# A projection issued one step earlier and a SiLU issued three steps later in a fused graph and Mamba kernel

## The reference

```python
h = layernorm(x) @ W_fc1.T + b_fc1
u, z = split(h @ W_in.T)                      # 1024 channels each
u = silu(causal_conv4(u) + conv_b)            # 4 taps along the tokens
dt, B, C = split(u @ W_xproj.T)               # 32, 16, 16
delta = softplus(dt @ W_dt.T + b_dt)
h[t] = exp(delta[t] * A) * h[t-1] + (delta[t] * u[t]) * B[t]     # 16 states per channel
y[t] = sum_s h[t, s] * C[t, s] + u[t] * D
x = x + (y * silu(z)) @ W_out.T @ W_fc2.T + b_fc2
```

## Time and profile before

| what | value |
|---|---|
| median of 3 runs (lowest, highest) | 3827.84 us (3824.13, 3829.54) |
| the profiled execution, its own time | 3826.3 us |
| its span, first to last instruction | 3824.5 us |
| VectorE busy, share of the span | 3570.9 us, 93% |
| TensorE matmul busy | 3473.0 us, 91% |
| GpSimd busy | 3453.5 us, 90% |
| ScalarE busy | 2853.9 us, 75% |
| mean granted TensorE clock | 0.985 of full |

### The profile page before, as it was taken

The page is one execution under the profiler, slowest core; times in us unless marked ns, Lnnn a source line. Parts: engine busy times, 40 slices in busy tenths (PEclk is TensorE's granted clock), DMA queues, the critical chain, the costliest instruction groups (busy, mean ns, idle before and its releaser), DMA issues.

```text
span 3824.5 us, 43807 instructions
## 1 busy us (share of the span) xinstructions
PE 3473.0 (91%) x11130; PEld 1956.7 (51%) x11130; DVE 3570.9 (93%) x3133; ACT 2853.9 (75%) x6066; POOL 3453.5 (90%) x1860
## 2 busy tenths in 40 slices
PE   6789999999999999999999999999999999999888
PEld 3645555555555555555555555555555555555444
DVE  0399999999999999999999999999999999999998
ACT  1487777887777877777878777778777778777774
POOL 0199999999999999999999999999999999999998
PEclk9899999999999999999999999999999999999999
DMA  2111101111101111101111100111110111110110
GB/s 105 56 54 57 57 7 54 54 57 57 57 8 52 54 57 57 57 16 44 54 57 57 57 36 24 54 57 57 57 51 10 57 54 57 57 53 9 45 50 9
DMA packets 50702, 183.68 MB, mean 48 GB/s; under 512 B 7339, under 2 KB 33203, under 8 KB 42067
## 3 DMA queue, kind: packets, MB, share of 16 engines
q1 hardware_dynamic: 48880, 174.17, 11.8%
q10 hardware_dynamic: 1636, 7.83, 0.5%
HBM read 164.15 MB, written 17.83 MB: 48 GB/s over the span
## 4 chain that ended last, share of the span: by engine, by line
POOL 53%; issue 32%; PE 8%; DVE 4%; ACT 1%; POOLq 1%; DMA 0%; SPq 0%; DVEq 0%; ACTq 0%
POOL st L409 35%; POOL st L400 10%; POOL du_sb L390 3%; POOL delta L382 3%; PE y_ps L680 2%; PE g L700 2%; DVE st L863 2%; DVE st L851 1%; POOL rstd L348 1%; PE dec L617 1%; POOLq L189 1%; DVE u L889 0%; PE g L822 0%; DMA rows<-bk_dram 0%; PE dec L626 0%
## 5 line engine op out<-in xcount | busy, mean ns | idle before, releaser
L409 POOL TENSOR_TENSOR st<-st,bc 128x1024 f32<-128x1024 f32 x1024 | 2402.7, 2360 | 183.4 <-DVE st L863 178.9
L863 DVE TENSOR_TENSOR_SCAN st<-dec,st 128x1024 f32<-128x1024 f32 x1024 | 2330.5, 2289 | 36.1 <-ACT dec L462 28.8
L680 PE MATMUL y_ps<-st,ident 128*128 128x512 f32 x4096 | 1950.0, 608 | 250.5 <-POOL st L409 246.4
L462 ACT ACTIVATE dec<-delta,decay 128x254 f32<-128x254 f32 x4096 | 1697.1, 464 | 479.6 <-DVE st L863 475.9
L680 PEld LDWEIGHTS y_ps<-st,ident 128*128 128x128 f32 x4096 | 743.5, 191 | 1096.7 <-issue 621.4
L851 DVE TENSOR_TENSOR st<-du,bc 128x1024 f32<-128x1024 f32 x736 | 893.7, 1214 | 0.7 <-ACT du L448 0.6
L400 POOL TENSOR_TENSOR st<-du_sb,bc 128x1024 f32<-128x1024 f32 x288 | 679.6, 2360 | 0.1
L502 ACT ACTIVATE u<-d_ps,bconv,chan 128x256 f32<-128x256 f32 x256 | 130.1, 558 | 338.5 <-PE d_ps L718 332.3
L889 DVE SCALAR_TENSOR_TENSOR u<-d_ps,chan,u 128x250 f32<-128x250 f32 (+2 forms) x768 | 307.4, 473 | 59.2 <-ACT u L502 59.2
L718 PE MATMUL d_ps<-xnT,wxz 128*128 128x256 f32 x1024 | 256.5, 396 | 9.5 <-DVE u L889 8.7
L730 PE MATMUL d_ps<-xnT,wxz 128*128 128x256 f32 x1024 | 246.3, 383 | 15.0 <-ACT zs L513 14.4
(11 more groups left out here) (101 smaller groups left out, 2459.0 us busy)
## 6 DMA issues: line engine op xcount, KB each, us to landing
bc<-bc_dram SPq DMA_DIRECT2D x64, 2048.0 KB, 9.4
xg<-x_dram SPq DMA_DIRECT2D x32, 256.0 KB, 11.4
x_dram<-xg SPq DMA_DIRECT2D x32, 256.0 KB, 2.0
last_x<-x_dram SPq DMA_DIRECT2D x32, 256.0 KB, 2.6
out_dram<-last_x SPq DMA_DIRECT2D x32, 256.0 KB, 2.1
bc<-w_inT_dram ACTq DMA_DIRECT2D x1, 4096.0 KB
adjt<-adjT_dram SPq DMA_DIRECT2D x32, 128.0 KB, 11.1
bc<-w_out_dram ACTq DMA_DIRECT2D x1, 2048.0 KB
```

What stands on the lines that cost most here:

```text
L409: nc.gpsimd.tensor_tensor(st[:, sl, :, :, :], st[:, sl, :, :, :], bc[:, p, 1, SU * q:SU * q + SU, None, :].to_broadcast([P, SU, 2, T]), AL ...
L462: a = nc.scalar.activation(dec[:, v % 2, s, j, :].rearrange("p (b t) -> p b t", b=PAIR)[:, :, 1:], delta[:, p, 2 * i + j, :].rearrange("p ...
L680: mm = nc.tensor.matmul(y_all, ident[:, :], st[:, sl, s, :, :].rearrange("p j t -> p (j t)"), start=False, stop=(q == Q - 1 and s == SU - ...
L863: nc.vector.tensor_tensor_scan(h, dec[:, v % 2, :, :, :].rearrange("p s j t -> p (s j t)"), h, 0.0, ALU.mult, ALU.add).then_inc(S["scanned ...
```

## The change

u(0) of a group moves on TensorE from step 0 of a body to the end of step 31 of the body before, ahead of sum(30). It keeps its two waits. evac(i) and taps(i) keep their steps, for which a tuple `U_READY` of its own now stands. ScalarE's SiLU of z moves from step 3 to step 6, where it stands behind decays(7); step 7 begins with evac(3). No instruction is added or removed.

```diff
-U_STEPS = (0, 2, 4, 6)
+U_STEPS = (-1, 2, 4, 6)
+U_READY = (1, 3, 5, 7)
...
-SILU_U, SILU_Z = 10, 3
+SILU_U, SILU_Z = 10, 6
...
                 for v in range(U):
-                    if dense and v - 1 in U_STEPS:
-                        evacuate_u(act, k + 1, r, U_STEPS.index(v - 1))
+                    if dense and v in U_READY:
+                        evacuate_u(act, k + 1, r, U_READY.index(v))
...
                     if dense:
                         dense_pe(pe, k + 1, r, v, ends)
+                    if ends and v + 1 == U:
+                        first_u(pe, k + 2, p)
                     for step in graph_steps(k, p, v, ends, begins):
                         graph_pe(pe, *step)
...
+            def first_u(pe, g, r):
+
+                wait(pe, "xnT_made", g + 1)
+                wait(pe, "z_biased", J * g)
+                if isinstance(g, int) and g == 0:
+                    pe.wait_ge(S["folded"], FOLDS)
+                project_u(pe, g, r, 0)
+
+            def project_u(pe, g, r, i):
+
+                for j in (2 * i, 2 * i + 1):
+                    for c in range(KC):
+                        mm = nc.tensor.matmul(d_ps[:, j % 2, :], wxz[:, c, j * P:(j + 1) * P],
+                                              xnT[:, r, c, :], start=(c == 0), stop=(c == KC - 1))
+                mm.then_inc(S["u_mm"], 1)
+
             def dense_pe(pe, g, r, v, ends):
                 if v in U_STEPS:
-
                     i = U_STEPS.index(v)
-                    if i == 0:
-                        wait(pe, "xnT_made", g + 1)
-                        wait(pe, "z_biased", J * g)
-                        if isinstance(g, int) and g == 0:
-                            pe.wait_ge(S["folded"], FOLDS)
-                    else:
-                        wait(pe, "taps", CONV * g + 6 * i)
...
+                    wait(pe, "taps", CONV * g + 6 * i)
+                    project_u(pe, g, r, i)
...
             def conv(dve, g, r, v):
 
-                for i, start in enumerate(U_STEPS):
+                if v in U_READY:
                     for n in range(6):
-                        if v == start + 1:
-                            tap(dve, g, r, i, n)
+                        tap(dve, g, r, U_READY.index(v), n)
```

## The result

| what | before | after |
|---|---|---|
| median (lowest, highest) | 3827.32 us (3824.13, 3829.54), 4 runs | 3789.21 us (3787.34, 3790.81), 4 runs |
| profiled execution, its time (span) | 3826.3 us (3824.5) | 3789.18 us (3787.4) |

The ratio is 0.9901, 95% interval 0.9884 to 0.9918: 1% faster, against 3787 us forecast.

A forecast was written before the change was run, and what follows sets the result against it. VectorE's waits were taken to bound the kernel: 81.7 us before, 30 x 0.85 + 10 x 1.2 + 3.4 = 40.9 after. The 40.8 gain from 3826.3 gives 3785.5, plus 1.5 for the median: 3787 us, range 3768 to 3815.

The forecast's parts named there:

- VectorE sets the period: GpSimd waits for scans, level with VectorE at c(27), with at least 2.0 us to give; VectorE's savings shorten the period.
- u(0) fits ahead of sum(30): TensorE's idle 1.94 us ahead of sum(30) takes u(0)'s 1.89 without delaying that sum; gain 1.1 us at taps(0).
- The SiLU fits in step 6: ScalarE's table load and SiLU fit between decays(7) and evac(3); the 1.07 us wait at scan(5) goes.
- u(3) stops VectorE next: u(3) stays behind sum(4), which needs c(4); taps(3) waits 0.85 us, leaving VectorE a lead of about 1.35 us.
- The thin margins: taps(2), scan(8) and gate(0) hold by little: charged at nothing, each bounded at 0.3 us, 9 us over the bodies.
- The clock: TensorE's clock falls move ahead of sum(2), in about ten bodies; taps(3) comes 1.2 us later there than in other bodies.
- The last dense body: A clock fall at sum(4) holds taps(3), so nothing is gained there: 3.4 us of waits stay.
- The sum: VectorE's waits in the 31 bodies fall from 81.7 to 40.9 us, a gain of 40.8.

The follow-up runs named there:

- x_pad7: The changed kernel plus two spare statistics instructions on VectorE (0.65 us together) ahead of the taps of step 7; 3787.46 us, 0.9900 of the kernel before.
- e6_u3_ahead: The changed kernel with u(3) issued in step 5 ahead of sum(4), instead of step 6 behind it; 3789.33 us, 0.9907 of the kernel before.
- e2_silu_alone: The kernel before with only the SiLU moved to step 6, u(0) staying in step 0; 3786.43 us, 0.9901 of the kernel before.
- x_pad14: The changed kernel plus the same two spare VectorE statistics instructions, in step 14; 3820.83 us, 0.9986 of the kernel before.
- e1_u0_alone: The changed kernel with the SiLU back in step 3, so only u(0) is moved; 3792.31 us, 0.9919 of the kernel before.
- e7_out_spread: As e6_u3_ahead, plus the first block of the output projection in step 7 instead of 8; 3783.67 us, 0.9890 of the kernel before.
- e3_u2_step3: The changed kernel with u(2) on TensorE in step 3 ahead of sum(2), instead of step 4; 3792.26 us, 0.9914 of the kernel before.
- e9_hop_step3: The changed kernel with one graph hop on TensorE (6 matmuls, 1.3 us) moved from step 1 to step 3; 3779.65 us, 0.9881 of the kernel before.
- e10_hop_and_ahead: The hop move of e9_hop_step3 on top of e7_out_spread; 3761.72 us, 0.9834 of the kernel before.

## Why the prediction was right

- *VectorE sets the period.* Shown: spare work in step 14 costs at least its own length, and GpSimd still waits for scans.
- *u(0) fits ahead of sum(30).* It does, 0.23 us of idle are left ahead of the sum, and the wait at taps(0) is gone. The sum still starts with c(30), as forecast.
- *The SiLU fits in step 6.* It does; 2.0 us of ScalarE's idle time were forecast behind it, 2.09 measured. With the Trainium skill's figure for a table switch ("ScalarE: Activation LUTs", What ACT_TABLE_LOAD costs), about 1.3 us a body would have been lost; the trace shows no such drain, in step 6 as in step 7, and the measurement decides.
- *u(3) stops VectorE next.* 0.85 us forecast, 0.83 to 0.96 measured, and x_pad7 and e6_u3_ahead show that its place behind sum(4) is the cause. That c(4) alone sets that place is too simple: in the change the queue from sum(2) on, 2.64 us of waiting for c(2) behind it, reaches sum(4) at nearly the same moment. This is the step that made the forecast 3787 instead of some 3760.
- *The thin margins.* taps(2), scan(8) and gate(0) show no wait that the profile lists in ordinary bodies.
- *The clock.* Falls forecast in ten bodies ahead of sum(2): the ten of every third body and one more. Two sizes were off. The idle stretch is 2.64 us, not 1.95. The forecast's own rows give it: from 2127.1 to 2129.84 is 2.7 us, so the 1.95 was reckoned wrong, and the likeness to the 1.94 us that is filled was a slip too. And a fall costs 1.40 + 0.48 - 0.88 = 1.0 us more than an ordinary body, not 1.2. They hardly touch the sum, because only the count enters it. That the count stayed near ten was not understood: e2_silu_alone, e6_u3_ahead and x_pad14 have five, 29 and 19, at idle stretches that are the same or nearly so. The term 10 x 1.2 could as well have been 5 or 29 times, and the forecast was lucky in it: 29 falls would have put the time some 20 us higher.
- *The last dense body.* 3.4 us forecast to stay, because taps(3) hung on a fall at sum(4); 1.96 at taps(2) and 0.53 at gate(0) measured, and none at taps(3). The fall now comes at sum(2), so the reason given did not hold, and 0.9 us were gained.
- *The sum.* Forecast: waits from 81.7 to 40.9 us. Measured: 51.5 + 27.1 = 78.6 before (nineteen bodies wait 1.1 us at taps(0), not twenty, and one wait of 1.7 us of the 28.8 belongs to the start and stays) and 40.1 after, 38.5 us less, for 37.1 us between the two profiled executions.

What the prediction did not say, and e1 and e2 show, is that either part would have done. After the first one the cap of u(3) and the falls take nearly all that the second offers.

## What to carry to other kernels

When a wait on the bounding engine is removed, look for the next thing that this engine will meet and that does not move with it: here u(3) behind sum(4), which let VectorE keep 1.3 of the 2.17 us that it was early. Two edits that each gain up to the same cap are worth one of them; time them apart, and lift the cap before keeping both. Idle time that is filled on TensorE may open again a few steps later, so follow its queue to the next wait, and fill with work that waits for nothing itself: the moved hop took the falls away, the moved u(2) did not.

## What the runs showed of the hardware

The idle stretch alone does not say how often TensorE's clock falls. With about 2.6 us of idle ahead of sum(2) in every loop body, it fell in 10 bodies (x_pad7), 11 (the change), 13 (e1_u0_alone), 19 (x_pad14) and 29 (e6_u3_ahead and e7_out_spread). The falls keep a rhythm of bodies: every third one in the change, every fifth in e2_silu_alone, every second in the later part of e3_u2_step3, and every one in e6_u3_ahead and e7_out_spread, where the bodies follow at 112.6 to 112.7 us. What differs between the runs with equal stretches is the period of the bodies. That the period sets the rhythm is an inference; no run changed the period by itself.

The falls in the loop bodies follow idle stretches of 1.95 to 2.66 us and none of 1.35 us, and a sum behind a fall takes up to 3.68 us instead of 1.98. Why a given body falls was only seen, not explained; that no stretch above 1.5 us is left in steps 0 to 5 of e9_hop_step3 and e10_hop_and_ahead, and no fall in their loop bodies either, is what the runs show. The Trainium skill ("TensorE: Matmul & The Clock Gate", Part 1: The HAM clock gate) ties the clock to how busy TensorE has been; by that rule, the trace agrees.
